# Layer 3's attention: the heads normalised on VectorE, one tensor_scalar a head, instead of on GpSimd, two broadcast products per four heads

## What is computed

```python
def _ln(x, w, b):
    mu = jnp.mean(x, axis=-1, keepdims=True)
    var = jnp.mean(jnp.square(x - mu), axis=-1, keepdims=True)
    return (x - mu) * jax.lax.rsqrt(var + EPS) * w + b
...
q = _fp8_linear_pertensor(ln_out, wq, wq_scale, q_in_scale).reshape(b, s, g, hpg, d)
q = _ln(q, qln_w, qln_b)
k = _fp8_linear_pertensor(ln_out, wk, wk_scale, k_in_scale).reshape(b, s, g, d)
k = _ln(k, kln_w, kln_b)
v = _fp8_linear_pertensor(ln_out, wv, wv_scale, v_in_scale).reshape(b, s, g, d)
core = _gqa(q, k, v).reshape(b, s, nh * d)
```

## Time and profile before

| | |
|---|---|
| median of 3 runs | 3629.47 us (3626.36 to 3630.97) |
| the profiled execution | 3626.52 us |
| its span, first to last instruction | 3624.6 us |
| TensorE's matmuls, busy | 2732.7 us, 75% |
| VectorE, busy | 2035.2 us, 56% |
| ScalarE, busy | 1292.5 us, 36% |
| GpSimd, busy | 1139.3 us, 31% |
| mean granted clock of TensorE | 0.868 of 2.4 GHz |

### The profile page before, as it was taken

How to read it: one execution, slowest core, us unless ns; L and a number is a source line. 1 busy time by engine, 2 the same in 40 slices (tenths; PEclk the granted TensorE clock), 3 DMA queues, 4 the chain that set the end, 5 groups by cost and what they waited for, 6 DMA issues and landing times. The chain is left out here.

```text
span 3624.6 us, 47300 instructions
## 1 busy us (share of the span) xinstructions
PE 2732.7 (75%) x15337; PEld 1867.1 (52%) x15402; DVE 2035.2 (56%) x3817; ACT 1292.5 (36%) x2917; POOL 1139.3 (31%) x1056
## 2 busy tenths in 40 slices
PE   3875238548999576794788888867888887499998
PEld 2331114235777342673455555535555555487776
DVE  4763786455133354334788888756777776423332
ACT  0664426400121154111455555535555554111110
POOL 4441025100001341301665555515554452320000
PEclk9998558867599698797999999979999998699999
DMA  3332005302300234001000000100000000210001
GB/s 93 94 109 83 0 26 148 102 2 104 122 0 0 64 103 138 18 1 71 1 0 0 0 0 0 47 29 4 4 3 3 3 3 1 83 32 1 1 1 24
DMA packets 82008, 137.76 MB, mean 38 GB/s; under 512 B 19840, under 2 KB 63168, under 8 KB 76096
## 3 DMA queue, kind: packets, MB, share of 16 engines
q1 hardware_dynamic: 81856, 135.79, 12.0%
HBM read 76.45 MB, written 23.72 MB: 28 GB/s over the span
## 5 line engine op out<-in xcount | busy, mean ns | idle before, releaser
L474 DVE TENSOR_REDUCE a_mraw<-a_first_ps 128x4 f32<-128x1024 f32 (+1 forms) x256 | 309.1, 1220 | 126.4 <-PE a_first_ps L324 126.0
L381 ACT ACTIVATE a_et<-a_second_ps 128x1024 f32<-128x1024 f32 x256 | 262.4, 1025 | 157.9 <-PE a_second_ps L342 155.9
L1423 DVE TENSOR_TENSOR f3e_gated<-f3e_silu,f3e_u_ps 128x512 f32<-128x512 f32 x96 | 66.0, 687 | 304.3 <-PE f3e_s_ps L1374 202.6
L1404 ACT ACTIVATE f3e_silu<-f3e_g_ps 128x512 f32<-128x512 f32 x96 | 57.4, 598 | 397.4 <-PE f3e_g_ps L1361 397.4
L1383 PE MATMUL f3e_y_ps<-f_w,f3e_hidden 128*128 128x256 f32 x768 | 181.4, 380 | 1.9
L359 PE MATMUL a_o_ps<-a_et,a_vt 128*32 128x256 f32 x2048 | 167.1, 399 | 11.1 <-ACT a_osb L410 9.7
L342 PE MATMUL a_second_ps<-a_qs,a_ks 64*128 64x256 bf16 (+2 forms) x896 | 117.4, 296 | 59.0 <-ACT a_et L381 54.9
L1383 PEld LDWEIGHTS f3e_y_ps<-f_w,f3e_hidden 128*128 128x128 f32 x768 | 146.6, 191 | 18.4 <-DVE f3e_hidden L1426 1.2
L2594 ACT ACTIVATE a3x_weights<-a3x_s_ps,a3x_nmax 128x128 f32<-128x128 f32 x256 | 90.7, 368 | 165.0 <-DVE a3x_nmax L2707 165.0
L2594 ACT ACTIVATE a3o_weights<-a3o_s_ps,a3o_nmax 128x128 f32<-128x128 f32 x256 | 90.7, 368 | 157.7 <-DVE a3o_nmax L2707 157.7
L324 PE MATMUL a_first_ps<-a_ks,a_qs 64*128 64x256 bf16 (+2 forms) x1280 | 122.6, 265 | 31.5 <-DVE a_mraw L474 17.5
(11 more groups left out here) (557 smaller groups left out, 7129.6 us busy)
## 6 DMA issues: line engine op xcount, KB each, us to landing
f1w_w<-in_f_w SPq DMA_DIRECT2D x16, 1216.0 KB, 7.1
a_qs<-a_parts SPq DMA_DIRECT2D x144, 128.0 KB, 2.4
a_od<-a_osb SPq DMA_DIRECT2D x16, 1024.0 KB, 3.9
a_ks<-a_parts SPq DMA_DIRECT2D x96, 128.0 KB, 2.5
f_w_raw<-in_f_w SPq DMA_DIRECT2D x25, 256.0 KB, 2.7
a_zr<-a_zd SPq DMA_DIRECT2D x24, 256.0 KB, 3.6
a_oc<-a_od SPq DMA_DIRECT2D x64, 64.0 KB
a_od<-a_osb SPq DMA_DIRECT2D x8, 512.0 KB, 2.9
```

Source lines behind the costliest of these rows:

```text
L381: self.nc.scalar.activation(self.et[:, g % self.WAVES_HELD, :, :], self.second_ps[:, :, :], ACT.Exp, scale=self.scale).then_inc(self.e_rea ...
L474: v.tensor_reduce(out, self.first_ps[:, g % 2, :, :].rearrange("p u (c n) -> p u c n", n=N), AX.X, ALU.max).then_inc(self.max_taken, 1)
```

## The change

`center` goes from GpSimd to VectorE. There it is four instructions a group, one tensor_scalar a head, that subtract `mu[:, h]` and multiply by `dev[:, h]` as [P,1] scalars. Its first group waits for `dev_ready`, a new semaphore that `inverse` frees on GpSimd. `deviation` loses its wait for `centered`, and `inverse` gets it. In `order()` two of the six groups stay at the head of the step, the others stand further back.

```diff
-        order = center(0, 1, 2, 3, 4, 5)
-        order += (scores(0) + [("a", "exponential", 0)] + rows("rows") + values(0) + values(1) + normalise(0))
-        order += (scores(1) + turn(0) + [("a", "exponential", 1)] + project(0) + apply(0) + statistics(0)
+        order = center(0, 1)
+        order += (scores(0) + [("a", "exponential", 0)] + rows("rows") + values(0) + values(1) + center(2)
+                  + normalise(0))
+        order += (scores(1) + turn(0) + [("a", "exponential", 1)] + project(0) + apply(0) + center(3) + statistics(0)
                   + normalise(1) + project(1) + round_(0) + rows("turn"))
-        order += (scores(2) + turn(1) + [("a", "exponential", 2)] + statistics(1) + project(2) + apply(1)
+        order += (scores(2) + turn(1) + [("a", "exponential", 2)] + center(4, 5) + statistics(1) + project(2) + apply(1)
...
                         pool.wait_ge(var_ready, at_batch(b, 1, 1))
+                        wait(pool, centered, at_batch(b, L, 0))
                         nc.gpsimd.tensor_tensor(dev[:, :], var[:, :], minus_half[:, :], ALU.pow)
                         nc.gpsimd.drain()
-                        nc.gpsimd.tensor_tensor(dev[:, :], dev[:, :], w_scale[:, 0, :], ALU.mult)
-                        nc.gpsimd.drain()
-
-                    def center(b, m):
-                        r = self.TURN_ORDER[m]
-                        heads = raw[:, parity(b), 4 * r:4 * r + 4, :]
-                        nc.gpsimd.tensor_tensor(heads, heads,
-                                                mu[:, 4 * r:4 * r + 4].unsqueeze(2).broadcast_to([P, 4, HEAD]),
-                                                ALU.subtract)
-                        nc.gpsimd.drain()
-                        nc.gpsimd.tensor_tensor(heads, heads,
-                                                dev[:, 4 * r:4 * r + 4].unsqueeze(2).broadcast_to([P, 4, HEAD]),
-                                                ALU.mult).then_inc(centered, 1)
+                        nc.gpsimd.tensor_tensor(dev[:, :], dev[:, :], w_scale[:, 0, :], ALU.mult).then_inc(dev_ready, 1)
...
                     def deviation(b, k):
                         v.drain()
 
-                        wait(dve, centered, at_batch(b, L, 0))
...
+                    def center(b, m):
+                        r = self.TURN_ORDER[m]
+                        if m == 0:
+                            dve.wait_ge(dev_ready, at_batch(b, 1, 1))
+                        for h in range(4 * r, 4 * r + 4):
+                            head = raw[:, parity(b), h, :]
+                            mm = v.tensor_scalar(head, head, mu[:, h:h + 1], dev[:, h:h + 1], ALU.subtract, ALU.mult)
+                        mm.then_inc(centered, 1)
```

More of the change, by code:

```diff
@@ L2364, in run @@
             var_ready = sem("var_ready")
+            dev_ready = sem("dev_ready")
             centered = sem("centered")
@@ L2482, in quantise @@
                             mm.then_inc(xq_ready, 1)
-                    steps(pool, {("p", "inverse"): inverse, ("c", "center"): center, ("r", "quantise"): quantise})
+                    steps(pool, {("p", "inverse"): inverse, ("r", "quantise"): quantise})
                 @block.tensor
@@ L2745, in _ @@
                                 ("p", "statistics"): statistics, ("p", "deviation"): deviation,
+                                ("c", "center"): center,
                                 ("a", "maximum"): maximum, ("a", "normalise"): normalise,
```

## The result

The changed kernel takes 3766.31 us (3758.68 to 3770.12), beside it the kernel before 3630.22: 1.037 times as long, with an interval of 1.035 to 1.039. The profiled execution took 3764.31 us, 137.8 more than that of before. The forecast was 3720, with a range up to 3760: the direction and the mechanism held, the size was 46 us short, and the measured time lies 6 us above the range.

A forecast was written before the change was run, and what follows sets the result against it. No engine is full; a chain between VectorE, ScalarE and TensorE bounds the step. 14 x 3.65 (cross) + 14 x 3.3 (own) = 97, -8 for first steps, +3 for last: +92 us, so 3720, range 3642 to 3760.

The forecast's parts named there:

- the wait: Head of VectorE's queue: center(0) waits for dev until t 4.65; scores 1 starts at 8.45 instead of 2.87, TensorE loses 5.6 us.
- The signs that the prediction had named: VectorE idle 4.2 us, TensorE 5 to 6 before scores 1; slow matmuls; rounding 0 in 2.7. Wrong if heads' pitch off.
- What is given back: Faster rounding 0 and slack leave +2.0 us at maximum 2; behind it +2.0 stays in the cross, +1.6 in the own pass.
- Behind maximum 3 nothing changes: Step's end: statistics 4 and 5, rounding 3 and deviation stay as before, so the delay goes whole into the next step.
- The relief rival: VectorE's rounding 0 stays slowed, not due to the centring: 104 us more, over 3800; chance 0.04.
- the free clock: Rival: TensorE's clock behind the idle before scores 1 costs nothing; +45, 3673 us; chance 0.20.
- faster: Rival: VectorE's own queue sets maximum 2, 0.5 us less than before; 3602 us, needing a delay under 0.2 a step; chance 0.06.
- Halving the width takes off what it takes off bn_stats: Heads on VectorE: from pitch 0.324 us at width 256, take off 0.13; 0.19 a head, 4.6 us a step.
- cheap heads: Rival: 0.12 us a head on VectorE, at L1528's rate; 3688 us with the clock's cost, 3642 without; chance 0.08.
- The rival of heads that don't overlap: VectorE's heads at 0.27 us each, the 16 on the path costing 1.3 us more a step: +36, 3755; chance 0.08.
- The first centred step has no attention beside it ...: -4 in each pass: Start of each pass: TensorE's three waits for GpSimd, 4.8 us, go away but for some tenths.
- The clock: TensorE slow after idling: 2.0 us more for scores 1, turn 0, project 0; 1.65 of it arrives at maximum 2.

## Why the prediction was off by 46 us

What bounds the kernel, and the wait. Right: a step is set by the chain from maximum over ScalarE to TensorE, and delaying maximum 0 delays all. The wait measured 4.27 us for 4.2, scores 1 came at t 8.91 for 8.45, TensorE idled 5.89 us for 5.6. The signs that the prediction had named came, and so did one that it had named as a sign of being wrong: the heads' pitch is off.

What is given back. Right: rounding 0 in 2.69 us for 2.70, and TensorE's wait for it gone. Not quite right: "Behind maximum 3 nothing changes". In the own pass maximum 3 came 4.6 us later and the step grew by 4.4, but in the cross pass it was 5.7 and 5.0: 0.7 us came back, since the key projections no longer fell into a slow phase (64.1 us before, 53.3 after, 0.8 a step). The relief rival, the free clock and "faster" (which needed a delay under 0.2 us a step) are out.

The table's sums against the terms: 14 own steps at 4.44 instead of 3.3 and 14 cross steps at 4.96 instead of 3.65 are 34 us; the first intervals, -0.6 and +3.7 where I had -4 each, are 11. That makes 45 of the 46. The remaining 3 us of the 138 are what I had put down for the last steps with heads, but no run separates them.

- **The heads' pitch: 27.6 us, shown.** In the traces, too, the steps give 25.7 us and the first intervals 2.0. It is what 0.061 us a head is worth; for the whole difference of 0.257 to 0.19 I estimate 30. The step that failed is "Halving the width takes off what it takes off bn_stats". It took 0.13 off 0.324; the true figure is 0.067. I read 0.324 us at 256 elements as a rate of 1.04 ns with a small fixed part; it is 0.52 ns and a large one, 0.06 for each [P,1] scalar. L1528's 0.6 ns an element had the right rate and lacked the scalars. The rule of the Trainium skill (VectorE: DVE Perf Modes, The perf-mode tier table) of twice the base rate agrees with these pitches; I had set it aside, and its result, cheap heads, was wrong nevertheless, since the rate was not what cost. The rival of heads that don't overlap had the pitch nearly right (0.27), and with it the time (3755), for a wrong reason: a duration is 0.339 us and the pitch 0.257, so the heads do overlap. The rule of the Trainium skill (VectorE: DVE Perf Modes, The DRAIN you can't avoid), that an instruction starts only when the one before has left the pipe, doesn't describe these rows. The same section of the Trainium skill lets an instruction that isn't held start earlier, and the row of 0.257 agrees with that.
- **The first interval: 7.0 us in the traces, shown.** (8.6 by the medians.) The step that failed is "The first centred step has no attention beside it ...: -4 in each pass". The new wait stands there too, and I listed the row task as hidden "in that gap", which exists only beside an attention. Here nothing else kept TensorE busy. The pitch makes 2 us of the 11, and 2 stay open.
- **The clock: 4 us of miss.** 1.65 a step had been put down, 50 / 28 = 1.79 was measured. At maximum 2 it was 1.85 and 2.49 in the mean, and 2.7 in the step shown, as in the row that I had discounted; 0.1 and 0.6 of it were given back behind maximum 3. I was near in part by two errors that cancelled.
- Of the steps' 34 us some 2 stay unexplained, if the pitch is taken whole (28 in the steps, an estimate) and the clock at 4.

## What to carry to other kernels

When work moves to another engine, ask first where its wait will stand in the new engine's queue: here one wait for a 4.2 us power, placed 4.3 us before its answer was there, cost 198 us and turned a gain of 1.7% (in a kernel that doesn't divide by the deviation) into a loss of 3.7%; with the groups behind maximum 1 dev was there when they came, and the change gains 2.0%. What a wait costs depends on what stands around it: the same one cost 135 us in the kernel before. Price a short instruction from rows of its own form, with its kinds of operands, at two widths, so that fixed part and rate come apart, before scaling one of them. And follow each moved task to the ends of the pipeline, where the cover that hides it in the steady step is missing.
